# One attention half, its batches put into four phases and its transposes into row halves, on one Trainium2 core

## The reference

```python
def xattn(v, k, q, mask, ...):            # q = layernorm(x), k = v = ctx
    qh, kh, vh = heads(q @ wq + bq), heads(k @ wk + bk), heads(v @ wv + bv)
    logits = einsum('bhqd,bhkd->bhqk', qh, kh) / sqrt(D) + mask * -1e9
    out = einsum('bhqk,bhkd->bhqd', softmax(logits), vh)
    return merge(out) @ wo + bo
x = x + tanh(g_xattn[0]) * xattn(ctx, ctx, layernorm(x), mask, ...)
x = x + tanh(g_ffn[0]) * ffn(layernorm(x), ...)
```

## Time and profile before

| | us |
|---|---|
| median of 3 runs | 1243.25 |
| lowest and highest | 1242.18 and 1249.38 |
| the profiled execution | 1245.54 |
| its span, first to last instruction | 1243.8 |
| busy in the span: PE, DVE, ACT, POOL | 1188.9, 902.1, 620.0, 550.7 |

### The profile page before, as it was taken

One profiled execution on the slowest core, in us unless ns is written; L12 is line 12 of the kernel. 1 busy time (PEld: TensorE's weight loads), 2 busy tenths in 40 slices (PEclk: granted clock), 3 DMA queues, 4 the chain that ended last, 5 costly groups with the idle time before them and its releaser, 6 DMA issues. The chain is left out here.

```text
span 1243.8 us, 41871 instructions
## 1 busy us (share of the span) xinstructions
PE 1188.9 (96%) x16568; PEld 947.7 (76%) x16568; DVE 902.1 (73%) x2556; ACT 620.0 (50%) x1481; POOL 550.7 (44%) x821
## 2 busy tenths in 40 slices
PE   5699999999999999999879999999999999999995
PEld 4477777777777777777557888888888888888874
DVE  3477777777877777777757877777877777787763
ACT  3366666666666666665434444434444444443431
POOL 3476777677777767777611122122122212212120
PEclk9899999999999999999999999999999999999998
DMA  8899998888778878877315656656666665665663
GB/s 229 193 203 199 207 201 201 178 187 185 179 179 186 183 177 186 178 175 159 69 50 127 163 140 145 152 140 149 148 157 142 137 167 145 142 155 139 148 149 94
DMA packets 263010, 200.31 MB, mean 161 GB/s; under 512 B 195934, under 2 KB 243872, under 8 KB 258720
## 3 DMA queue, kind: packets, MB, share of 16 engines
q1 hardware_dynamic: 262816, 197.64, 70.2%
HBM read 125.49 MB, written 72.11 MB: 159 GB/s over the span
## 5 line engine op out<-in xcount | busy, mean ns | idle before, releaser
L899 POOL TENSOR_SCALAR shifted<-raw,neg_max 112x375 f32<-112x375 f32 x512 | 327.3, 649 | 163.5 <-DVE neg_max L781 120.3
L781 DVE CUSTOM_DVE_ANT_0 raw<-bank_s,maskb 112x375 f32<-112x375 f32 x512 | 266.6, 544 | 103.0 <-issue 87.8
L686 ACT ACTIVATE probsT<-bank_t 128x512 f32<-128x512 f32 (+3 forms) x512 | 189.1, 458 | 104.1 <-PE bank_t L460 104.1
L447 PE MATMUL bank_s<-K_stack,Q_stack 128*112 128x375 bf16 x512 | 150.8, 335 | 5.0 <-DVE neg_max L781 4.7
L1444 DVE TENSOR_REDUCE max<-bank_s 112x4 f32<-112x448 f32 x128 | 78.8, 615 | 71.6 <-PE bank_s L1201 71.6
L460 PEld LDWEIGHTS bank_t<-ident,shifted 48*128 48x128 f32 (+1 forms) x3072 | 105.3, 139 | 27.8 <-issue 24.2
L460 PE MATMUL bank_t<-ident,shifted 48*128 48x48 f32 (+1 forms) x3072 | 122.6, 226 | 0.0
L1537 POOL TENSOR_TENSOR mix_bd<-pm_te,tok 128x448 f32<-128x448 f32 x32 | 31.5, 986 | 200.5 <-DMA pm_te<-pm_dram 200.5
L1153 PE MATMUL bank_ab<-xnT,wq2T 128*128 128x224 f32 x512 | 109.4, 357 | 0.7 <-ACT qT L1337 0.6
L1153 PE MATMUL bank_ab<-xnT,wk2T 128*128 128x224 f32 x512 | 109.6, 357 | 0.0
L203 POOL TENSOR_SCALAR var_eps<-moments 112x1 f32<-112x1 f32 x32 | 7.2, 224 | 227.0 <-DVE moments L199 226.8
(11 more groups left out here) (147 smaller groups left out, 2191.8 us busy)
## 6 DMA issues: line engine op xcount, KB each, us to landing
K_stack<-k_dram SPq DMA_DIRECT2D x64, 562.5 KB, 7.8
k_dram<-k_parts SPq DMA_DIRECT2D x32, 562.5 KB, 4.4
att_dram<-att_q SPq DMA_DIRECT2D x31, 511.0 KB, 3.9
att_th<-att_dram SPq DMA_DIRECT2D x31, 511.0 KB, 4.3
v_dram<-mv SPq DMA_DIRECT2D x32, 455.0 KB, 6.5
v<-v_dram SPq DMA_DIRECT2D x32, 455.0 KB, 4.0
K_stack<-k_dram SPq DMA_DIRECT2D x32, 375.0 KB, 9.2
Q_stack<-q_dram SPq DMA_DIRECT2D x64, 168.0 KB, 9.1
```

Source lines behind the costliest of these rows:

```text
L447: nc.tensor.matmul(bank_s[h % 2][0:S, 0:S2], Q_stack[:, p, h, :], K_stack[:, p, h, :], start=True, stop=True).then_inc(scores_ready, 1)
L686: act.activation(probsT[:, g % 2, first_u:end, lo:hi], bank_t[0:KP, bank, column:column + (end - first_u) * (hi - lo)].rearrange("p (u q) ...
L781: dve.tensor_tensor_reduce(raw[:, g % 2, j, :], bank_s[h % 2][0:S, 0:S2], c.maskb[:, :], -1.0, -LEAST, ALU.add, ALU.min, neg_max[:, g % 2, ...
L899: pool.tensor_scalar(shifted[:, g % 2, j, 0:S2], raw[:, g % 2, j, :], -1.0, neg_max[:, g % 2, j:j + 1], ALU.mult, ALU.add).then_inc(shift_ ...
```

## The change

Transposes of context, x, heads and back are split into two row halves of 64 (`turn_halves`), one per bank of `bank_ab`, as the probabilities are already. For that `xn` and `heads` get 128 rows whose tails are set to zero once, `heads` holds the heads as two halves, `wo` is loaded in four pieces to match, and the copies on ScalarE (`ctxT`, `xnT`, `outT`) gather from both banks.

`body(b)` on TensorE becomes four sections. Each has four scores with full-array matmuls between them, then a turn of probabilities with one of the other turns behind it, then a weighing. `body(b)` now begins with score 4 of batch b and ends with scores 0 to 3 of b+1, and context and x of b+3 are turned together near its end; keys and queries are still of b+2. The keys wait for both copies, ctxT and xnT.

The other engines follow that order. SyncE stores q ahead of k, and loads x of one batch (112 KB) per body from batch 4 on, in place of four batches (448 KB) in each of the first seven.

```diff
+            def turn_halves(columns, width, src, f):
+                for r in range(2):
+                    rows = slice(r * HALF, (r + 1) * HALF)
+                    last = nc.tensor.transpose(bank_ab[0:f.stop - f.start, r, columns:columns + width], src[rows, f], c.ident[rows, rows])
+                return last
...
-                        last = nc.tensor.transpose(bank_ab[:, e, k * KP:(k + 1) * KP],
-                                                   ctx_in[:, p, k, e * P:(e + 1) * P], c.ident[0:KP, 0:KP])
+                        last = turn_halves((e * KC + k) * HALF, HALF, ctx_in[:, p, k, :], slice(e * P, (e + 1) * P))
...
-                    last = nc.tensor.transpose(bank_ab[0:S, 0, g * P:(g + 1) * P], headsT[:, g * S:(g + 1) * S], c.ident[:, :])
+                    last = turn_halves(g * HALF, HALF, headsT, slice(g * S, (g + 1) * S))
...
                 if t == 0:
                     pe.wait_ge(ctxT_copied, b + 1)
+                    if b >= 2:
+                        pe.wait_ge(xt_copied, b + 1)
...
+            def body(b):
...
+                S_(b, 4, 5)
+                if b + 2 < B:
+                    keys(b + 2, 0, 0)
+                S_(b, 6)
+                if b + 2 < B:
+                    queries(b + 2)
...
+                S_(b, 7)
+                turn(b, 0, b == 0)
+                if back:
+                    weigh(b - 1, 1 - p, NG - 1, False)
+
+                S_(b, 8, 9)
+                if b + 2 < B:
+                    keys(b + 2, 1, 0)
+                S_(b, 10, 11)
+                turn(b, 1, b == 0)
...
+                    heads_back(b - 1)
+                weigh(b, p, 0, b == 0)
+
+                S_(b, 12, 13)
...
+                        pe.wait_ge(heads_done, b)
...
+                    values(1 - p, 0)
+                    values(1 - p, 1).then_inc(va_ready, 1)
+                S_(b, 14, 15)
+                turn(b, 2, False)
...
+                    heads_turn(b - 1)
+                weigh(b, p, 1, False)
+
+                S_(b + 1, 0, 1)
...
+                    values(1 - p, 2).then_inc(vb_ready, 1)
                 else:
-                    open_x(b + 2 - B)
+                    open_proj(0)
+                S_(b + 1, 2)
                 if back:
                     project(b - 1)
+                S_(b + 1, 3)
+                if b + 1 == B:
+                    open_proj(1)
+                turn(b, 3, False)
+                if b + 3 < B:
+                    turn_ctx(b + 3)
+                    turn_x(b + 3)
+                elif b + 1 < B:
+                    open_x(b + 3 - B)
+                weigh(b, p, 2, False)
...
-                act.activation(ctxT[:, p, :, :], bank_ab[:, :, 0:SK], ACT.Copy).then_inc(ctxT_copied, 1)
+                act.activation(ctxT[:, b % 2, :, :].rearrange("p e (k r s) -> p r (e k) s", r=2, s=HALF),
+                               bank_ab[:, :, 0:X_AT].rearrange("p r (n s) -> p r n s", s=HALF), ACT.Copy).then_inc(ctxT_copied, 1)
...
+            def load_x(b):
+                g, n = b // z.GX, b % z.GX
+                if b == z.GX:
                     sp.wait_ge(wt_ready, len(turns))
+                if n:
+                    sp.wait_ge(c.x_loaded[g], 16 * n)
+                sp.dma_start(c.X[0:S, b:b + 1, :], d.x[b:b + 1].rearrange("b s e -> s b e")).then_inc(c.x_loaded[g], 16)
...
+            pool.memset(xn[:, :], 0.0)
+            pool.memset(heads[:, :, :, :], 0.0).then_inc(tails_set, 1)
```

More of the change, by code:

```diff
@@ L267, in cross @@
     HALVES = ((0, LOW), (LOW, z.S))
+    HALF = P // 2
+    X_AT = EC * KC * HALF
     o = c.o
@@ L519, in open_gates @@
                 for t in range(EC):
-                    last = nc.tensor.matmul(bank_ab[0:S, 0, 0:2 * z.H2 * z.X], o.xnT[:, t, e, :], c.wgT[:, t, :], start=(t == 0), stop=(t == EC - 1))
+                    last = nc.tensor.matmul(bank_ab[0:S, 1, 0:2 * z.H2 * z.X], o.xnT[:, t, e, :], c.wgT[:, t, :], start=(t == 0), stop=(t == EC - 1))
                 last.then_inc(o.gates_ready, 1)
@@ L529, in open_proj @@
                 last.then_inc(o.proj_ready, 1)
-            def body(b, p, i, first, ahead, last):
-                back, front = not first, not last
-                S_ = lambda *hs: [scores(b, p, i, h, first) for h in hs]
-                if ahead:
-                    transposes(b + 2, i + 1, p)
-                S_(0, 1)
-                if back:
-                    weigh(b - 1, 1 - p, NG - 2, False)
-                    turn(b - 1, NG - 1, False)
-                S_(2, 3)
-                if ahead:
-                    keys(b + 2, p, 0)
-                S_(4)
+            def body(b):
+                p = b % 2
+                back = b > 0
+                S_ = lambda n, *hs: [scores(n, n % 2, n // 2, h, n == 0) for h in hs if n < B]
+                S_(b, 4, 5)
[4 more added lines that the diff above has]
+                    queries(b + 2)
+                elif b + 2 == B:
+                    open_gates(0)
+                S_(b, 7)
+                turn(b, 0, b == 0)
@@ L546, in body @@
                 if back:
                     weigh(b - 1, 1 - p, NG - 1, False)
-                S_(5, 6)
-                if ahead:
-                    keys(b + 2, p, 1)
-                S_(7)
-                if last:
-                    pe.wait_ge(o.gates_copied, 1)
-                if back:
-                    if ahead:
-                        pe.wait_ge(k_copied, 2 * (EC * (b + 2) + 1))
-                    heads_back(b - 1)
-                S_(8)
-                turn(b, 0, first)
-                if ahead:
-                    pe.wait_ge(k_copied, 2 * EC * (b + 3))
@@ L615, in _ @@
             turn_weights(0, 1)
-            transposes(1, 0, 1)
+            turn_ctx(1)
             turn_weights(2, 3)
-            keys(1, 1, 0)
+            keys(1, 0, 0)
             keys(1, 1, 1)
@@ L628, in _ @@
             pe.wait_ge(v_copied, 2)
-            batches(pe, body)
-            weigh(B - 1, 1, NG - 2, False)
-            open_proj(0)
-            turn(B - 1, NG - 1, False)
+            for h in range(G):
+                scores(0, 0, 0, h, True)
+            for b in range(B):
+                body(b)
             weigh(B - 1, 1, NG - 1, False)
-            pe.wait_ge(o.xt_copied, 2)
+            pe.wait_ge(x_done, B - 1)
             heads_back(B - 1)
-            open_proj(1)
             heads_turn(B - 1)
@@ new lines, in out_copy, with open_x_copy @@
+                act.activation(outT[:, :, :].rearrange("p e (r s) -> p r e s", r=2),
+                               bank_ab[:, :, 0:EC * HALF].rearrange("p r (e s) -> p r e s", e=EC), ACT.Copy).then_inc(outT_copied, 1)
+            def open_x_copy(e):
+                act.wait_ge(o.xt_ready, e + 1)
+                for r, (lo, hi) in enumerate(HALVES):
+                    last = act.activation(o.xnT[:, :, e, lo:hi], bank_ab[:, r, X_AT:X_AT + EC * HALF].rearrange("p (e s) -> p e s", e=EC)[:, :, 0:hi - lo], ACT.Copy)
+                last.then_inc(o.xt_copied, 1)
@@ L881, in _ @@
             key_third(1, 1)
-            split_queries(1)
+            query_rest(1)
+            split_rest(1)
+            moments_of(2)
             copy_weights(*range(7, len(turns), 2))
-            batches(dve, body)
+            normalise_x(2)
+            score_max(0, True, 0, 1, 2, 3)
+            for b in range(B):
+                body(b)
             dve.wait_ge(o.consts_done, 2)
@@ L951, in _ @@
                 add_bias(b)
-            batches(pool, body)
+            inverse_deviation(2)
+            add_bias(2)
+            shift(0, 0, True)
+            for b in range(B):
+                body(b)
 def switch(nc, z, d, c):
```

350 lines of the change are left out of this document (176 added, 174 removed).

## The result

The changed kernel is slower. In 20 runs of each kernel on one chip its median is 1255.36 us (1246.19 to 1260.31) against 1246.43 us (1241.91 to 1254.7): a ratio of 1.0056, 95% interval 1.0039 to 1.0072. 1228.4 was forecast, with a range of 1218 to 1250, and the median lies outside it. It does so too on a common base: the 20 runs of the kernel before lie 3.2 us above the three that the forecast was taken off, which would make it 1231.5 and the range's end 1253.2. The profiled execution took 1253.81 us around a span of 1251.7, so 7.9 us more span than before.

What follows compares the result with a forecast made beforehand. TensorE was taken to bound the first half; 29 periods falling from 18.085 to 17.65 us save 12.6, the tail 2.3, together 14.9 off the 1243.25 us median: 1228.4, range 1218 to 1250.

Steps and rivals of the forecast that it cites:

- The blocks: TensorE's own work in a first-half batch: its blocks were to sum to 17.43 us instead of 18.085.
- Turning by halves: TensorE's 14 full transposes a batch become pairs of halves at 0.074 us each: -0.54 us a batch.
- The four phases: Four round trips a batch between full-array and tiled matmuls on TensorE instead of five: -0.12 to -0.14 us.
- rival 4: Transposed halves do not overlap on TensorE: 0.148 us a pair, 1258 us in all, chance 0.05.
- Keys late by 0.15: TensorE's first keys wait for ScalarE's ctxT and xnT copies: 0.15 us late a batch, bounds 0 and 0.55.
- Score 2 late by 0.07: VectorE's third key part stands ahead of the next batch's scores 0 and 1, making TensorE's score 2 0.07 us late.
- rival 2: Gain mostly hidden as stacks or ctxT come late by some tenths: period 17.9 to 18.0, 1236 to 1239 us, chance 0.25.
- The exchange: Key store and stack loads, third key part to last stack, take L = 16.3 us; period bound 17.0, under the forecast 17.65.
- x hides: Loading x batch by batch has the same bytes, stands behind Q in the DMA queue, and so costs nothing.
- rival 3: Queue crowding makes the key store take 6.7 us throughout: period 19.4, slower at about 1279 us, chance 0.07.
- The tail: End of the first half: the opening's second projection moves up ahead of the last turn, saving 2.3 us, bounds 0 and 4.
- The start: Before the steady batches: memsets, split wo loads and the new store order were not priced; bound 3 us either way.

Runs made afterwards that it cites:

- e8: Changed kernel with the key store ahead of the q stores, key parts made earlier, and ctxT and xnT copies divided between ScalarE and VectorE: 0.9843 of the kernel before.
- e3: Changed kernel with the copies of ctxT and xnT divided, lower row halves on ScalarE, upper on VectorE: 1.0079 of the kernel before.
- e1: Changed kernel with GpSimd's rest of the keys and VectorE's third key part made earlier: 0.9994 of the kernel before, 1.0025 when run again.
- e2: Changed kernel with x loaded in groups of four batches again, as in the kernel before: 1.0206 of the kernel before.
- e6: Changed kernel with the key store ahead of the q stores and the load of x behind them: 1.0052 of the kernel before.
- e9: As e8, with the load of x one batch further on, behind the q stores: 0.9835 of the kernel before, 1255.2 us.
- e7: Changed kernel with the key store ahead of the q stores and key parts made earlier: 0.9939 of the kernel before.
- group 1: Four variants on one chip: e1, e2, e3, and e1 with e3 (1.0015 of the kernel before); the kernel before has a median of 1280.16 us there.
- group 2: Four runs on a second chip: changed kernel again (1.0102 of the kernel before), key store put ahead of q stores (1.0055), e6 and e7; kernel before 1252.06 us.
- group 3: Three runs on a third chip: e1 again (1.0025 of the kernel before), e8 and e9; the kernel before has a median of 1274.56 us there.

## Why the prediction was wrong

*The blocks* came out right in the sum, 17.43 us forecast and 17.42 where the keys wait for nothing and the stacks come in time (e8), but by two errors that cancel, and so by luck. Turning by halves was to save 0.54; from start to start it saves 0.37: context and x 0.60, heads back 0.37 and heads 0.22, 1.19 in place of 1.56. The four phases were to save 0.12 and brought some 0.28, nearly all of it on the turns of probabilities, 3.34 a batch in place of 3.64. The halves do overlap (0.38 for the six pairs of the context, 0.063 each, where 0.074 was taken), which rules out rival 4. What was misread is the step out of a turn: "Going from a turn to a weighing shows no price (0.89, like other turns)", but the other turns had such a step behind them too. The changed kernel has turns without one, and they take 0.78: the step costs about 0.1 us, and x, whose four halves stand ahead of a weighing, pays it in place of the turn. So the prediction's reading that the trace "shows no drain there" does not stand. The rule of the Trainium skill (TensorEngine Tiling (Array Packing), Tiling Modes), that a change of tiling mode drains TensorE, agrees with the changed kernel's trace (0.78 against 0.89).

*Keys late by 0.15* was mis-sized: 0.31 to 0.32 (306.60 to 306.92, and 0.32 off the quiet batch in e3). The copies take what was taken for them, 0.81 and 0.38, although their pattern is new. The step that failed is where the first one starts: "0.20 after the context's turn ends". In the changed code `ctx_copy` waits for the turn of x as well, so it starts behind 305.53 and not behind 305.31, at 305.69 in place of 305.51. The wait stood in the code and was overlooked. Besides, the keys start 0.14 behind the end of xnT (306.78), for which the prediction had nothing; an overlap of the two copies by 0.10 and a longer turn of x (0.22 for 0.15) take back about as much.

*Score 2 late by 0.07* was right in its mechanism: the third key part does stand ahead of the scores' maxima. The size is 0.12 in the row of 320.72, and e1, which moves that part away, has quiet batches 0.16 shorter.

So the quiet period is 17.43 + 0.31 + 0.16 = 17.90 instead of 17.65. That alone would have made about 1236, the time of rival 2.

*The exchange* is the step that turned the sign: L = 16.3, so a bound of 17.0, "0.65 below 17.65". Measured by the medians of 200 to 500 us: key store 4.7 where 4.3 was taken, 9.9 for the last Q load where 9.5 was; from the first K load to the start of that Q load 2.6 (median of 26 batches) where 2.4 was. That makes 17.3 with the queue's 0.1, and 17.8 in the batch at 319.38. The key part ends 0.74 behind score 0 where 0.70 was taken (the prediction's own terms give 2.92 and so 0.75, not 2.87 and 0.70). The bound is then 18.0 at the median and 18.5 in that batch, above the quiet period. No term was off by more than a tenth, but all were off in one direction, and 0.65 was all the margin. The durations came from the kernel before, with a DMA share of 0.83 in place of 0.87; what lengthens each is not shown. That "x hides" is not contradicted: without its loads (e2) the store lands no sooner, and their place in the queue makes no difference (e6, e9).

This is the mechanism of rivals 2 and 3, "decides from L = 16.95 and makes the kernel slower from 17.4": at 17.3 to 17.8 it does the first, and the second in the batches that wait. The price of rival 3, a key store of 6.7 throughout, was too high.

*Waits without a releaser* are the second loss over the quiet period, and the prediction had no term for them: four of 0.4 to 2.2 us, with what the clock takes behind the longest (below). In the changed kernel's profile the 28 batches are 13.6 us longer than 28 quiet ones: some 7 us go to these four waits and the clock behind them, some 6 to the waits for `Q_stack`. In its second profile it is some 6 of 17, and some 11 for `Q_stack`. So the 20 us between the forecast of the first layer's periods (-12.6) and the measurement (+7.8) are 7 for the quiet period, 6 for the exchange and 7 for these waits. That e7 gains 20 us on the changed kernel while such waits stay (4.6 us in the one, 3.9 in the other) shows the part of the exchange; the part of these waits is read from the traces alone.

*The tail*, -2.3, measured -2.5. *The start*, 0 with 3 either way, measured +0.3. *The second layer unchanged* holds for its code, not for its time: the low clock that the tail left behind came to stand in it (below).

## What to carry to other kernels

If an order of work moves a consumer a quarter of a period forward, add up the round trip that feeds it from the durations of the loaded queue, and take the margin as gone where it is no more than the spread of the terms: here 0.65 us against three terms that grew by 0.2 to 0.4 each. A transfer on a critical round trip should be ready early and stand first in its queue: first alone gave 0.24 us a batch, early alone let the store land in 7.5 us in place of 4.7, both together gave 0.61. A block saved on the engine that is no longer the bound is given back at the next wait, so read quiet batches and mean batches apart: the first shows what the change did, the second what binds.

## What the runs showed that was not expected

Some waits of TensorE have no releaser in the profile. The two longest of the changed kernel stand in the middle of a weighing, three and two records before its end; the second is followed by a low clock (the window shows PEclk as the third number from the end):

```profile
247.00 0.38 PE L488 MATMUL bank_o<-probsT,V 128*32 128x112 f32 x3 [1.79 <-issue]
...
521.84 0.58 PE L488 MATMUL bank_o<-probsT,V 128*32 128x112 f32 x2 [2.23 <-issue]
...
522.00:524.00 2.00, 2.00 (x7) 1.40 (x7) 0.95 (x4) 0.00 (x0) 0.23 (x1) 0.50 0.83 225
```

They stand in the 10th and the 25th batch, which take 19.90 and 21.94 us: 2.0 and 4.0 over the quiet 17.90, in the second case because the blocks behind the wait ran at the 1.2 GHz level (0.50): four matmuls of the values take 1.71 us (523.02 to 524.73) in place of 0.86. In the second profile of the same kernel the longest batches are the 9th, behind a wait of 2.0 us for `Q_stack`, and the 25th, at the same place in the weighing as here. In the kernel before no such wait of TensorE's matmuls stands in the first layer. The packets of the traces point to a cause. The page of the profile lists a queue q8 of kind "instruction", 135 transfers in the changed kernel; each is of 16 KB, and between 60 and 640 us one comes about every 9 us. In the twelve profiles of the changed kernel and its variants 66 waits of 0.2 us or more have no releaser in the first layer, and all 66 end 1.3 to 1.8 us after such a transfer has landed. TensorE then seems to wait for its own code. The kernel before has 63 of these transfers there and no such wait; why they come late in the changed kernel stays open, and no run tests it.

In the second layer, whose code is the same, TensorE's wait for `mix_bd` between 700 and 1150 us was 1.9 us in the changed kernel's profile, 15.2 to 19.4 in the four of group 1, 2.9 to 8.3 in the four of group 2, and 13.7 to 17.0 in the three of group 3. It goes with the chip rather than with the edits; the profile of the kernel before has none, and on the other chips that kernel's own was not seen.

The gain of the tail was half a loan. Windows around the end of the first layer, first of the kernel before, then of the changed one (PEclk is the third number from the end):

```profile
626.00:628.00 2.00, 0.50 (x20) 0.50 (x24) 0.00 (x0) 1.45 (x4) 0.00 (x0) 1.00 0.01 4
628.00:630.00 2.00, 1.25 (x17) 0.70 (x10) 0.25 (x1) 1.03 (x2) 0.00 (x0) 0.91 0.00 0
630.00:632.00 2.00, 2.00 (x4) 0.71 (x3) 0.43 (x2) 0.00 (x0) 0.00 (x0) 0.50 0.00 0
632.00:634.00 2.00, 1.55 (x5) 0.64 (x4) 0.00 (x0) 0.70 (x2) 0.00 (x0) 0.74 0.00 0
```

```profile
636.00:638.00 2.00, 0.77 (x12) 0.53 (x12) 0.68 (x2) 0.17 (x2) 0.00 (x0) 0.97 0.00 0
638.00:640.00 2.00, 1.66 (x4) 1.06 (x4) 0.00 (x0) 0.28 (x1) 0.00 (x0) 0.50 0.00 0
640.00:642.00 2.00, 1.15 (x3) 0.68 (x3) 1.21 (x6) 0.23 (x1) 0.00 (x0) 0.50 0.00 0
642.00:644.00 2.00, 2.00 (x6) 1.60 (x6) 1.89 (x8) 0.39 (x1) 0.83 (x2) 0.50 0.00 0
```

Before, TensorE had waited much from 624 to 630, the clock fell to 0.50 (the 1.2 GHz level), and the second projection of the opening ran at it: 3.27 us. Moved up into the busy stretch it costs 1.81 (630.28 to 632.09). The low clock comes all the same, after the waits of 634 to 638, and now falls on the last projection (2.04 against 1.12 before) and on the opening of the second layer: from its first block to its next of the same kind 6.56 us (641.24 to 647.80) where before had 4.85 (635.68 to 640.53). That is 1.7 of the second layer's 2.3.
